# A two-layer graph network on one core: gathered tiles in two groups of seven instead of three groups of five

## The chip, the cores and the metric

One core of a Trainium2 chip runs the whole kernel. The metric is the device time in microseconds (us) of one execution, as the median of several runs; one further execution was profiled, and its trace is what the rows below come from. Engines are called as in the profile: PE (TensorE; PEld is its weight load), DVE (VectorE), ACT (ScalarE), POOL (GpSimd), SP (SyncE).

## What is computed

The graph has 12,500 nodes with 128 features and 412,500 edges, sorted by their target. Cut to what matters, the reference is:

```python
h = relu(layernorm(x))                       # layer 0
msg = where(edge_type == 0, h[src] @ W_data.T + b_data, h[src] @ W_ctrl.T + b_ctrl)
x = x + relu(segment_sum(msg, dst) + h @ W_self.T + b_self)
h = relu(layernorm(x))                       # layer 1
x = x + segment_sum((h @ W_in.T)[src], dst) + deg[:, None] * (h @ W_out.T)
```

The kernel sums the features of the source nodes first and multiplies by the weights afterwards, once per target node. What costs time is the sum over the edges.

## The kernel before, in words

**Tables.** The features of a layer are held as three bf16 parts (high, middle, low) of 128 columns each, 384 columns per node, in HBM (`tables[l]`) and in SBUF (`tab`). Nodes are taken in 98 blocks of 128; edges lie in tiles of 128, some 33 of them per block.

**Two ways of summing.** The first blocks of a layer (`GATHERED`: 56 in layer 0, 38 in layer 1) are summed by gathering. For each tile of 128 edges POOL issues an indirect DMA (L580) that brings 128 rows of 384 columns from the table into `rows`; DVE builds a 0/1 matrix `hot` that says which edge goes to which target (`make_hot`, L1130); PE multiplies the three parts by it and accumulates in `bank_g` (`add_group`, L667: three matmuls per tile, six where a tile straddles two pairs of blocks). The planner has 1,860 gathered tiles in layer 0 and 1,266 in layer 1. The other blocks are summed densely: DVE marks rows and columns (`mark`, L1142 and L1144), PE turns the marks into a 128-column strip of an adjacency matrix (`build`, L720), ACT copies it out (L961), and PE multiplies the matrix with the table in SBUF (`dense`, L737, 98 matmuls of 384 columns for each half block in layer 0, or block in layer 1).

**Steps.** All engines run through the same list of steps, in program order and without a scheduler: 16 steps for each dense sum, 1,360 steps in layer 0 and 976 in layer 1, and some before and behind. In a step PE does first the gathered groups that are due, then small turns and the ends of finished blocks, then one build and about six dense matmuls. A planner (`Plan`) spreads the groups evenly over the steps: `due[g] = 8 + g * (S - 12) // groups`. DVE builds the `hot` of a group three steps ahead of its due step, before it makes the marks of that step.

**Groups and ring.** Gathered tiles are handled in groups of `GROUP` = 5: one `make_hot` per group, one wait of PE per group for the landing of its gathers, one semaphore update after its last matmul (`s.added`). `rows` and `hot` have room for `RINGS` = 3 groups. POOL waits before a group until the group three before it was added; DVE waits likewise in `make_hot`:

```python
for g in range(plan.groups):                                   # POOL, L573
    while n < len(plan.fetch) and plan.fetch[n][0] - 4 <= plan.due[g]:
        fetch(n)
        n += 1
    if g >= RINGS:
        pool.wait_ge(s.added, g - RINGS + 1)
    for t in plan.group_tiles(g):
        pool.indirect_dma_start(...)                           # L580
```

**Other work in those queues.** POOL also fetches the edge list of a block (`fetch`, L565: 98 in layer 0, 60 in layer 1). DVE unpacks a list at step f (`unpack`, L1154 to L1177), and for a dense block PE turns it in step f + 1 (`turn_list`, L685). At the first step of each dense sum PE waits until ACT has copied the last sum out of `bank_d` (L735, L899). A general path (for graphs that the windows don't cover) is in the code and isn't taken here. Between the layers POOL waits for all stores of layer 0, and layer 1 starts with its own gathers.

**What follows from the due steps.** The step at which a pair of blocks ends (`pair_step`, one after the due step of its last group), the fetches and the ends of blocks are placed by the due steps too.

Of the kernel before, what the change touches and what calls it, by code (L numbers as in the profile page):

```python
# [7 lines left out]
def gnn_kernel(nc, x, src, dst, etype, w_data, b_data, w_ctrl, b_ctrl, w_self, b_self, w_in, w_out, out):  # L8
# [30 lines left out]

    GATHERED = (NB * 28 // 49 // 2 * 2, NB * 19 // 49 // 2 * 2)  # L40
    KINDS = (2, 1)
    GROUP, RINGS = 5, 3
    PACKS = 4
    MARKS, AHEAD = 4, 2

# [1274 lines left out]
```

How the kernel before makes its waits and increments, by code:

```python
        def wait(eng, semaphore, n):  # L386
            eng.wait_ge(semaphore, n)
            if not isinstance(n, int):
                eng.sem_inc(s_apart[eng.engine], 1)
# [1 line left out]
        def either_path(eng, fast, general):  # L391
            eng.wait_ge(s_covered, 1)
            with eng.If(eng.value_load(covered[0:1, 0:1], min_val=0, max_val=1) == 1):
                fast()
            with eng.Else():
                general()
# [4 lines left out]
        @block.sync  # L401
        def _(sp):
            sp.wait_ge(s_x_pad, 1)
            for c in range(XCH):
                n0, n1 = XB[c], min(XB[c + 1], NB - 1)
                sp.dma_start(tab_x[:, n0:n1, 0:F],
                             x[n0 * P:n1 * P, :].rearrange("(n p) f -> p n f", p=P)).then_inc(s_x[c], 16)
            sp.dma_start(tab_x[0:LAST, NB - 1, 0:F], x[(NB - 1) * P:N, :]).then_inc(s_x[XCH - 1], 16)
            pk_rows = pk.rearrange("(c p) e -> p c e", p=P)
            sp.wait_ge(s_edges[0], PIECES)
            sp.dma_start(pk_rows[:, :, 0:P], raw[0].rearrange("p (c e) -> p c e", e=P)).then_inc(s_packed, 16)
            sp.wait_ge(s_edges[3], PIECES)
            sp.dma_start(pk_rows[:, :, P:P + HALF],
                         nxt_i.bitcast(fp32).rearrange("p (c e) -> p c e", e=HALF)).then_inc(s_packed, 16)
            sp.wait_ge(s_pay, 2)
            pay = raw[2].rearrange("p (c e) -> p c e", e=P)
            sp.dma_start(pk_rows[:, :, P + HALF:2 * P + HALF], pay).then_inc(s_packed, 16)
```

## Time and profile before

| what | us |
|---|---|
| median of 3 runs | 4440.64 |
| lowest and highest run | 4433.56 and 4442.63 |
| the profiled execution's own time | 4440.43 |
| span of its instructions | 4438.4 |
| around the span | 2.0 |

By the profile's busy shares PE was busy for 92% of the span, DVE for 79%, POOL for 72%, ACT for 53%, and the DMA engines for about a third. A share is an average over stages: layer 0 runs from about 190 to 2747 us, layer 1 from about 2750 to the end, and they have to be read apart. POOL's share leaves out the time between two of its DMA instructions, which the profile calls "issue".

### The profile page before, as it was taken

To read this page: it belongs to the slowest core of one execution; us is meant where nothing else is said; L and a number is where in the kernel's file an instruction comes from. 1 tells how busy PE (TensorE), PEld (TensorE's weight loads), DVE (VectorE), ACT (ScalarE), POOL (GpSimd) and SP (SyncE) were. 2 spreads that over 40 slices of the span, in tenths; PEclk is the share of its full clock that TensorE was granted. 3 is DMA by queue.
4 is the path that set the end of the run, shared out by engine and by line. 5 is a ranking of instruction groups with operands and counts; after the bars stand their busy time and mean duration, and the time that the engine had idled before them with its cause. 6 is when DMAs were issued, how large, how long until landed. Compare 5 with 4: busy or idle time off the path is not lost.

```text
span 4438.4 us, 102927 instructions
## 1 busy us (share of the span) xinstructions
PE 4103.0 (92%) x42000; PEld 2506.4 (56%) x42000; DVE 3509.9 (79%) x8092; ACT 2334.0 (53%) x3663; POOL 3188.3 (72%) x3360
## 2 busy tenths in 40 slices
PE   0399999999999999999999996999999999999999
PEld 0255555555555555555555554566656565656665
DVE  5678777787788778778777875888888888888886
ACT  4445555555555555555555553555555555555554
POOL 4377777777777777777777775777777777777776
PEclk9599999999999999999999998999999999999999
DMA  7223333333333333333333334433333333333332
GB/s 198 73 82 91 94 88 89 93 91 90 89 90 93 90 90 92 90 92 90 91 89 92 90 89 118 124 93 91 91 93 91 91 93 91 91 91 94 90 90 78
DMA packets 289371, 417.62 MB, mean 94 GB/s; under 512 B 70913, under 2 KB 228895, under 8 KB 288895
## 3 DMA queue, kind: packets, MB, share of 16 engines
q0 software_dynamic: 160160, 338.57, 27.1%
q1 hardware_dynamic: 121784, 66.09, 5.2%
q10 hardware_dynamic: 6951, 6.30, 0.6%
q8 instruction: 336, 5.51, 0.5%
q14 instruction: 140, 1.15, 0.1%
HBM read 373.52 MB, written 37.20 MB: 93 GB/s over the span
## 4 chain that ended last, share of the span: by engine, by line
PE 53%; POOL 24%; issue 9%; DVE 8%; ACT 3%; ACTq 1%; DMA 0%; POOLq 0%; DVEq 0%; SPq 0%
PE bank_d L737 33%; POOL arena L580 23%; PE bank_g L667 10%; PE banks_m L720 8%; DVE arena L1144 1%; POOL arena L565 1%; DVE arena L1142 1%; ACT arena L961 1%; ACT arena L899 1%; DVE arena L1130 1%; ACT arena L862 1%; ACTq L824 1%; PE bank_a L694 0%; PE bank_b L703 0%; DVE tab L1053 0%
## 5 line engine op out<-in xcount | busy, mean ns | idle before, releaser
L580 POOL DMA_INDIRECT arena<-table,idx x3126 | 2971.9, 951 | 1023.3 <-issue 924.1
L737 PE MATMUL bank_d<-tab,arena 128*128 128x384 bf16 x14112 | 2696.4, 328 | 36.1 <-ACT arena L899 35.1
L961 ACT ACTIVATE arena<-banks_m 128x784 bf16<-128x784 f32 x2304 | 1912.2, 830 | 1511.4 <-PE banks_m L720 1457.3
L737 PEld LDWEIGHTS bank_d<-tab,arena 128*128 128x128 bf16 x14112 | 1196.5, 98 | 955.3 <-issue 263.6
L1142 DVE TENSOR_TENSOR arena<-iota_ps,arena 128x256 bf16<-128x256 f32 (+1 forms) x2304 | 1220.6, 530 | 335.4 <-PE banks_m L720 302.9
L1144 DVE TENSOR_TENSOR arena<-iota_ps,arena 128x392 bf16<-128x392 f32 x2304 | 1279.4, 555 | 0.0
L720 PE MATMUL banks_m<-arena 64*128 64x98 bf16 (+1 forms) x13056 | 808.1, 226 | 49.7 <-ACT arena L961 36.3
L667 PE MATMUL bank_g<-arena 128*128 128x192 bf16 (+29 forms) x12753 | 763.2, 212 | 24.8 <-DMA arena<-table,idx 23.0
L667 PEld LDWEIGHTS bank_g<-arena 128*128 128x128 bf16 x12753 | 709.7, 97 | 118.2 <-issue 27.1
L720 PEld LDWEIGHTS banks_m<-arena 64*128 64x128 bf16 x13056 | 352.2, 95 | 580.6 <-ACT arena L961 419.8
L1130 DVE TENSOR_TENSOR arena<-iota_ps,rel 128x960 bf16<-128x960 f32 (+1 forms) x626 | 592.0, 946 | 3.2
L1183 DVE TENSOR_TENSOR d_sum<-arena 128x128 f32<-128x128 f32 x144 | 42.5, 295 | 319.3 <-ACT arena L899 307.2
L565 POOL DMA_INDIRECT arena<-pk,list_at x158 | 150.1, 950 | 108.0 <-issue 74.6
L922 ACT ACTIVATE arena<-bank_a 64x128 f32<-64x128 f32 x204 | 55.5, 272 | 150.1 <-PE bank_a L686 146.9
L931 ACT ACTIVATE arena<-bank_a 128x128 f32<-128x128 f32 x196 | 54.4, 277 | 136.3 <-PE bank_a L694 132.7
L899 ACT ACTIVATE arena<-bank_d 128x384 f32<-128x384 f32 x144 | 70.8, 491 | 58.1 <-PE bank_d L737 58.1
L533 POOL TENSOR_TENSOR arena<-arena,tab 128x256 f32<-128x256 f32 x49 | 35.4, 726 | 80.5 <-ACT tab L866 75.6
L685 PE MATMUL bank_a<-ident,arena 128*128 128x128 f32 x102 | 30.4, 298 | 65.8 <-DVE arena L1177 65.8
L1201 DVE SCALAR_TENSOR_TENSOR arena<-bias,count,bank_b 128x128 f32<-128x128 f32 x98 | 33.8, 345 | 61.2 <-issue 56.7
L629 PE MATMUL banks_m<-ident,arena 128*128 128x128 f32 x30 | 6.8, 397 | 78.8 <-ACT arena L848 39.5
L1154 DVE SCALAR_TENSOR_TENSOR arena<-arena,node 128x192 f32<-128x192 int32 x158 | 64.8, 410 | 16.0 <-DMA arena<-pk,list_at 16.0
L694 PE MATMUL bank_a<-ident_b,tab 128*128 128x128 bf16 x588 | 65.0, 219 | 5.1 <-ACT arena L908 2.2
(133 smaller groups left out, 1594.6 us busy)
## 6 DMA issues: line engine op xcount, KB each, us to landing
arena<-table,idx POOLq DMA_INDIRECT x3126
table<-tab SPq DMA_DIRECT2D x7, 1344.0 KB, 5.6
table<-arena SPq DMA_DIRECT2D x98, 96.0 KB
tab<-table SPq DMA_DIRECT2D x7, 1344.0 KB, 17.1
x<-arena SPq DMA_DIRECT2D x98, 64.0 KB
arena<-x SPq DMA_DIRECT2D x98, 64.0 KB
arena<-in_x_dram SPq DMA_DIRECT2D x97, 64.0 KB
out_dram<-arena SPq DMA_DIRECT2D x97, 64.0 KB
```

Of the source, the lines that this page charges most:

```text
L565: pool.indirect_dma_start(out=pack[:, i % PACKS, :], out_offset=None, in_=pk, in_offset=bass.IndirectOffsetOnAxis(ap=list_at[:, m:m + 1], ...
L580: pool.indirect_dma_start(out=rows[:, g % RINGS * GROUP + t % GROUP, :], out_offset=None, in_=tables[l], in_offset=bass.IndirectOffsetOnAx ...
L667: last = pe.matmul(bank_g[p % 2][:, to:to + (c1 - c0) * y], rows[:, at, a * F:(a + 1) * F], hot[:, at, c0 * y:c1 * y], start=(a == 0 and p ...
L694: last = pe.matmul(bank_a[:, 0:P], mine[:, a * F:(a + 1) * F], ident_b[:, :], start=(a == 0), stop=(a == 2))
L720: last = pe.matmul(bank_m[hf][:, n * nc_:(n + 1) * nc_], is_row[at, s_ % MARKS, n, :], is_col[at, s_ % MARKS, n * nc_:(n + 1) * nc_], star ...
L737: last = pe.matmul(bank_d[:, 0:RW], adj[q % 2][:, b * P:(b + 1) * P], tab[:, b, :], start=(b == 0), stop=(b == NB - 1))
L899: act.activation(d_sb[:, :], bank_d[:, 0:RW], ACT.Copy).then_inc(s.dense_out, 1)
L961: act.activation((adj0, adj1)[l][q % 2].rearrange("p c (h d) -> p c h d", h=2)[:, :, :, n * j:n * j + n], banks_m[:, :, 0:n * nc_].rearran ...
L1130: dve.tensor_tensor(hot[:, at:at + n, 0:c], iota_w[:, 0:c].unsqueeze(1).to_broadcast([P, n, c]), (rel0, rel1)[l][:, ts[0]:ts[0] + n].unsqu ...
L1142: dve.tensor_tensor(is_row[:, s_ % MARKS, 0:n, :], iota_r.unsqueeze(1).to_broadcast([P, n, P]), rc[:, i % 2, 0, pr:pr + n].unsqueeze(2).to ...
L1144: dve.tensor_tensor(is_col[:, s_ % MARKS, 0:n * nc_].rearrange("p (n c) -> p n c", n=n), iota_c[l].unsqueeze(1).to_broadcast([P, n, nc_]), ...
L1154: after(dve.scalar_tensor_tensor(out=arena[:, V_AT:E_AT], in0=pack[:, k, 0:W3].bitcast(i32), scalar=node[:, m:m + 1], in1=pack[:, k, W3:2 ...
```

## The change

The change alters two constants. Tiles per group go from 5 to 7, groups in the ring from 3 to 2; the tiles in the ring go from 15 to 14.

```diff
     GATHERED = (NB * 28 // 49 // 2 * 2, NB * 19 // 49 // 2 * 2)
     KINDS = (2, 1)
-    GROUP, RINGS = 5, 3
+    GROUP, RINGS = 7, 2
     PACKS = 4
     MARKS, AHEAD = 4, 2
```

By the planner's formulas the groups go from 372 to 266 in layer 0 and from 254 to 181 in layer 1. The due steps lie 5 or 6 apart instead of 3 or 4. The last group of layer 0 has five tiles in both versions and is due at step 1350 instead of 1352; that of layer 1 has six tiles instead of one and is due at step 966 instead of 968. POOL and DVE wait for the group two before instead of three before. The number of gathers, of matmuls and of elements that DVE compares stays as it is.

## Rows read from the trace of the kernel before

**Rows 1.** Windows: start:end, length, busy us (instructions) by engine, PE clock, DMA.

```profile
300.00:2716.00 2416.00, 2347.59 (x21375) 1408.95 (x21376) 1921.15 (x4808) 1291.46 (x2028) 1780.81 (x1873) 1.00 0.32 90
3000.00:4400.00 1400.00, 1359.48 (x16572) 843.13 (x16570) 1169.41 (x2404) 757.45 (x1112) 1059.75 (x1117) 1.00 0.33 91
```

**Rows 2.** Groups by line, POOL, 300 to 2716 us: busy, mean ns | idle, releasers.

```profile
L580 POOL DMA_INDIRECT arena<-table,idx x1780 | 1693.5, 951 | 607.0 <-issue 516.8 <-PE bank_g L667 90.2
L565 POOL DMA_INDIRECT arena<-pk,list_at x93 | 88.3, 949 | 28.4 <-issue 28.4
```

**Rows 3.** The same, POOL, 3000 to 4400 us (layer 1).

```profile
L580 POOL DMA_INDIRECT arena<-table,idx x1068 | 1014.3, 950 | 325.6 <-issue 325.6
L565 POOL DMA_INDIRECT arena<-pk,list_at x49 | 46.5, 948 | 14.9 <-issue 14.9
```

**Rows 4.** Waits of PE, 300 to 2716 us: total us, times, longest us.

```profile
PE bank_a L685 <- DVE arena L1177: 26.6, 25, 2.4
PE banks_m L720 <- ACT arena L961: 20.0, 26, 0.8
PE bank_d L737 <- ACT arena L899: 19.6, 50, 0.7
```

**Rows 5.** Waits of PE, 2790 to 4400 us (layer 1), the longest.

```profile
PE bank_g L667 <- DMA arena<-table,idx: 23.0, 37, 1.6
```

**Rows 6.** Timeline of PE, layer 0, a step without and one with a group.

```profile
1503.35 0.34 PE L720 MATMUL banks_m<-arena 64*128 64x196 bf16 x4
...
1504.71 0.34 PE L720 MATMUL banks_m<-arena 64*128 64x196 bf16 x4
...
1505.97 1.40 PE L667 MATMUL bank_g<-arena 128*128 128x192 bf16 x15
1507.31 0.34 PE L720 MATMUL banks_m<-arena 64*128 64x196 bf16 x4
```

**Rows 7.** Groups by line and shape, DVE's make_hot: busy, mean ns | idle.

```profile
L1130 DVE TENSOR_TENSOR arena<-iota_ps,rel 128x960 bf16<-128x960 f32 x372 | 427.6, 1150 | 2.2
L1130 DVE TENSOR_TENSOR arena<-iota_ps,rel 128x480 bf16<-128x480 f32 x253 | 164.1, 649 | 0.9
```

**Rows 8.** Timeline, layer 0: hot, unpack of a list, PE's turn of it.

```profile
896.94 1.15 DVE L1130 TENSOR_TENSOR arena<-iota_ps,rel 128x960 bf16<-128x960 f32 x1
...
898.81 0.41 DVE L1154 SCALAR_TENSOR_TENSOR arena<-arena,node 128x192 f32<-128x192 int32 x1
...
900.87 0.29 DVE L1177 CAST arena<-arena 128x256 f32<-128x256 int32 x1
...
901.22 0.33 PE L685 MATMUL bank_a<-ident,arena 128*128 128x128 f32 x1 [0.48 <-DVE arena L1177]
```

**Rows 9.** Timeline, start of layer 1: gathers, third list fetch, first add, ring wait.

```profile
2752.97 0.95 POOL L580 DMA_INDIRECT arena<-table,idx  x1 [0.30 <-issue]
...
2771.79 0.98 POOL L565 DMA_INDIRECT arena<-pk,list_at  x1 [0.30 <-issue]
...
2774.00 1.38 PE L667 MATMUL bank_g<-arena 128*128 128x96 bf16 x15
...
2775.66 0.95 POOL L580 DMA_INDIRECT arena<-table,idx  x1 [2.89 <-PE bank_g L667]
```

**Rows 10.** Timeline, layer 1: last gather of a group, and its add.

```profile
3549.60 0.95 POOL L580 DMA_INDIRECT arena<-table,idx  x1 [0.31 <-issue]
...
3552.78 1.09 PE L667 MATMUL bank_g<-arena 128*128 128x22 bf16 x30
```

**Rows 11.** Waits of POOL, 2790 to 4400 us: ring waits after the first.

```profile
POOL arena L580 <- PE bank_g L667: 1.9, 3, 1.3
```

**Rows 12.** Timeline, end of layer 1: last gather and last two adds.

```profile
4416.24 0.95 POOL L580 DMA_INDIRECT arena<-table,idx  x1 [0.30 <-issue]
...
4417.73 0.52 PE L667 MATMUL bank_g<-arena 128*128 128x22 bf16 x15 [0.22 <-DVE arena L1130]
...
4422.17 0.22 PE L667 MATMUL bank_g<-arena 128*128 128x2 bf16 x3
```

## The prediction

> **What bounds the kernel now.** I read the windows first, one for each layer's steady stretch [rows 1]: PE is busy for 2347.6 of 2416 us in layer 0 (97.2%) and for 1359.5 of 1400 in layer 1 (97.1%), at full granted clock (1.00, the 2.4 GHz level). So both look bound by PE. The second view, POOL's groups by line, tells them apart. In layer 0 [rows 2] the busy and "issue" times of gathers and list fetches make 1693.5 + 516.8 + 88.3 + 28.4 = 2327 us, and 90.2 us more are waits for PE: the ring is full, PE sets the pace, POOL has 3.7% to spare. In layer 1 [rows 3] the same sum is 1014.3 + 325.6 + 46.5 + 14.9 = 1401 of 1400 us with no wait at all: here POOL is the bound, with (1014.3 + 325.6) / 1068 = 1.255 us per gather. PE's 2.9% of idle time there is the counterpart. The third view is PE's waits: in layer 0 [rows 4] none is for a gather, and the three named ones (lists from DVE 26.6 us, ACT's copies of strips 20.0, ACT's copy of a sum 19.6) are all there is; in layer 1 [rows 5] the longest is for gathers, 23.0 us in 37 waits. The change keeps the count of gathers, matmuls and compared elements, so it can only act through what is paid per group, through where a burst falls in the order, and through the depth of the ring.
>
> **Per group on PE: nothing.** In layer 0 a step without a group takes 1504.71 - 1503.35 = 1.36 us, one with a group 1507.31 - 1504.71 = 2.60 [rows 6], so five tiles cost 1.24 us, 0.083 for each of 15 matmuls. The 15 last 1.40 us from the first start to the last end, and the last alone is about 0.24 of that (1.40 less 14 x 0.083), so the group costs what its matmuls cost: switching to it and back takes 0 to 0.04 us. With 106 groups fewer in layer 0 that is 0 to -4 us; I take 0, because the pitch explains the whole 1.24. A group of seven then costs 7/5 x 1.24 = 1.74 us.
>
> **Per group on DVE.** 960 elements take 1150 ns and 480 take 649 [rows 7]: 1.044 ns an element and 148 ns for each instruction. Seven tiles take 148 + 1344 x 1.044 = 1.55 us in layer 0 (0.40 longer) and 0.85 in layer 1. DVE saves 106 x 0.148 = 15.7 us over layer 0 and 73 x 0.148 = 10.8 over layer 1. DVE is busy for 1921 of 2416 us in layer 0 [rows 1], so most of this is spare time that it gains, worth nothing. It reaches PE only where PE waits for DVE, at the lists [rows 4]. There a hot can stand just ahead of the unpack, in the same step of DVE: 1.15 us of hot, then marks, then the unpack, and PE waits 0.48 us for its end [rows 8]. That happens where a group is due three steps behind the unpack. By the planner's formulas this holds for 15 of the 41 lists behind the first in layer 0 now, and for 9 after the change. Hot ahead of an unpack thus goes from 15 x 1.15 = 17.3 us to 9 x 1.55 = 14.0. If all of that came through, PE would gain 3.3 us; I take half, **-1.5 us**. The bounds are -26.6 (all list waits go) and 25 x 0.40 = +10 (each of today's waits gets the longer hot).
>
> **Copies of the sums.** At the first matmul of a dense sum PE waits 19.6 / 50 = 0.39 us for ACT [rows 4], unless other work stands just before it. A group is due at that step in 22 of 83 cases now and in 16 after (planner), so six more waits come: **+2.3 us**. The strips' 20.0 us stay: DVE's marks and ACT's copies catch up while PE adds a group, for longer and less often.
>
> **The ring, layer 0.** A tile takes 2416 / 1780 = 1.357 us [rows 2], so seven take 9.5. Two groups before a slot is needed again are 19.0 us. In that time POOL must see the add end (0.28 us: 2774.00 + 1.38 to 2775.66, [rows 9]), issue seven gathers (8.78) and its share of list fetches (7 x 116.7 / 1780 = 0.46), the last must land, and PE must add (1.74). The landing isn't shown by itself; it is bounded by 0 and by the shortest time from the end of a group's last gather to its add, 3552.78 - 3550.55 = 2.23 us [rows 10]; I take 2.2. The sum is 13.5 of 19.0 us: 5.5 to spare, against 10.1 before (3 x 5 x 1.357 less 10.3). One or two list fetches of 1.25 us come at once, so 5.5 should do. POOL's waits for PE stay near 90 us, since PE sets the time: **0 us**.
>
> **The ring, layer 1.** POOL issues without a stop, so each wait for the ring goes straight to the end. After the last gather of a group POOL has 8.78 us of other gathers to issue; in that time PE must start the add (2.23 us later here), finish it (1.09 x 7/5 = 1.53), and be seen (0.28) [rows 10]. That is 4.0 us, 4.7 to spare. The latest case that I saw is the last add, 4422.17 - 4417.19 = 5.0 us behind its gather [rows 12]; with 1.8 on top it still leaves 2.0. So no wait in the steady stretch. At the start there is one. Two lists and 15 tiles now precede the third list at 2771.79, and POOL waits until 2775.66 [rows 9]. After the change 14 tiles end at 2752.97 + 14 x 1.255 = 2770.5 and the list at 2771.8; the first add of seven ends at 2774.00 + 1.93 = 2775.93, and POOL goes on at 2776.2, one tile and 0.55 us behind: +1.8. Of the later ring waits, 1.9 us in three [rows 11], about 1.0 is more than the usual gap of 0.3, and these go, since the next add is done before POOL has issued seven more. POOL's last gather so ends 0.8 later, at 4418.0. The tail gives it back: the last group has six tiles and is due two steps earlier. It lands by 4420.2, takes 0.52 x 6/5 = 0.62 us, and two steps of (4422.17 - 4418.25) / 4 = 0.98 us bring PE to 4422.8, against 4422.4 at the end of the last add now [rows 12]: **+0.4 us**.
>
> **Other edits.** DVE's wait for the ring is satisfied: it builds a hot three steps ahead of the due step, when the group two before, due 10 steps ahead, is long added. The first group needs seven tiles instead of five, 2.5 us later, and PE reaches its first add in layer 1 only some 15 us after five have been issued (2752.97 + 6.3 to 2774.00) [rows 9]. SP and ACT issue what they issued, the pair's copy moves by a step or two: 0.
>
> **Sum:** 4440.4 - 1.5 + 2.3 + 0.4 = **4441.6 us** for the profiled execution. This execution stands 0.2 us under the median of the runs, so I predict **4441.0 us**: no change that can be measured. About 0.2% (9 us) is what a measurement can tell from no change; the three runs differ by as much.
>
> **Rivals.** (a) *The longer hot lands on PE, slower.* Place: the lists of layer 0, L685. If hot stands in the way of most unpacks, each of the 41 lists costs 0.40 us more: +16.4 instead of -1.5, 4459 us. It decides once the step of the hot coincides with the unpack for more than today's 15. For it: these waits are the largest of PE in layer 0 [rows 4], and [rows 8] shows one. Against it: by the due steps there are 9. The Trainium skill (Perfetto Trace Analysis, section Optimizing Scalar/DVE Operations) says that where Vector is not saturated but causes bubbles on other engines, breaking instructions up may let work end sooner; by that rule this change goes the wrong way. The trace shows such bubbles, and not yet what their length hangs on. Chance 8%.
>
> (b) *The ring is too short, slower.* Place: POOL's wait before a group in layer 1. If PE's add comes later than 7 us behind the gather (8.78 less 1.8), POOL stops. Priced by what layer 0 shows: 90.2 us in some 356 groups [rows 2], 0.25 us a group, in 181 groups +45 us: 4486. For it: spare time halves. Against it: the 2.0 to 4.7 us above. The Trainium skill (Perfetto Trace Analysis, section Optimization Strategy) says that the same gap repeating on the engine that should be saturated can mean too few buffers; POOL shows no such gap in layer 1 now [rows 3], and no row here shows a ring of two. Chance 6%.
>
> (c) *DVE paces layer 0 more than its waits show, faster.* PE's waits for ACT's strips hang on marks, and marks on DVE. If the 15.7 us that DVE saves came through in full, in place of the -1.5: 4427 us. For it: 20.0 us of strip waits and 26.6 of list waits are there to be cut [rows 4]. Against it: DVE has 20% idle time. Chance 15%.
>
> (d) *Nothing moves.* The group costs PE nothing now, so the change could do just nothing: 4440.6 us. It lies inside the forecast.
>
> **How the numbers follow.** Forecast, with (d): 71%, with its own range from 4430 to 4451 (the bounds of the list waits are the widest term, and a few microseconds of them are likely). Of that, 65 points lie within 0.2%, 3 below and 3 above. Faster is then 15 + 3 = 0.18, slower 8 + 6 + 3 = 0.17, same 0.65. The range 4425 to 4456 takes in (c) and part of (a), and leaves out (b).
>
> **What would show it.** Right: 266 hots of about 1.55 us and 181 of 0.85; in layer 1 gathers at 1.255 us without waits for PE but the first, then some 4.4 us (2771.8 to 2776.2); in layer 0 PE without waits for gathers, list waits near 25 us, sum waits near 22. Wrong: POOL waiting for PE in the middle of layer 1, PE waiting for gathers in layer 0, or list or strip waits that change by over 10 us.

## The result, and the profile after

The changed kernel takes 4451.26 us (median; 4447.78 to 4456.20), the kernel before, run beside it, 4439.85 (4433.56 to 4442.63). The ratio is 1.0025, with a 95% interval from 1.0017 to 1.0034: **slower by 11 us**. That is inside the range from 4425 to 4456 and on the wrong side of "no change", by little: 0.25% against the 0.2% that was taken for the least that a measurement can tell. The profiled execution took 4448.05 us, 7.6 more than the profiled one of before. What the traces below account for is these 7.6 us, not the 11 of the medians.

The window of layer 0, and then POOL's groups by line (300 to 2716 us, then 3000 to 4400), against [rows 1 to 3]:

```profile
300.00:2716.00 2416.00, 2341.01 (x21339) 1402.30 (x21340) 1922.26 (x4700) 1285.38 (x2023) 1777.51 (x1871) 1.00 0.32 90
```

```profile
L580 POOL DMA_INDIRECT arena<-table,idx x1778 | 1690.7, 951 | 610.4 <-issue 516.1 <-PE bank_g L667 94.4
...
L580 POOL DMA_INDIRECT arena<-table,idx x1066 | 1012.7, 950 | 325.0 <-issue 325.0
```

Little moved on POOL. In layer 0 its waits for the ring went from 90.2 to 94.4 us, so PE still sets the pace. In layer 1, from 3000 us on, it waits for nothing, and a gather still takes (1012.7 + 325.0) / 1066 = 1.255 us. PE is where to look: in layer 0 it is busy for 6.6 us less in these 2416 than in [rows 1]. Its waits from 300 to 2716 us (total us, times, longest us), against [rows 4]:

```profile
PE banks_m L720 <- ACT arena L961: 26.1, 35, 1.6
PE bank_d L737 <- ACT arena L899: 24.0, 61, 0.4
PE bank_a L685 <- DVE arena L1177: 21.2, 14, 3.0
```

The same three waits stand there, in another order. Strips went from 20.0 to 26.1 us, sums from 19.6 in 50 waits to 24.0 in 61, lists from 26.6 in 25 to 21.2 in 14, with a longest of 3.0 instead of 2.4. There is no wait for a gather. DVE's `make_hot` by shape, against [rows 7], has the lengths that were worked out:

```profile
L1130 DVE TENSOR_TENSOR arena<-iota_ps,rel 128x1344 bf16<-128x1344 f32 x265 | 410.9, 1550 | 2.4 <-DVE cells L1216 0.2
L1130 DVE TENSOR_TENSOR arena<-iota_ps,rel 128x672 bf16<-128x672 f32 x180 | 152.7, 848 | 0.3
```

**What an uncovered sum costs.** The timeline of PE holds an ordinary step without a group and, behind it, the first step of a dense sum without one (start, us, instruction, idle time before it):

```profile
822.66 0.34 PE L720 MATMUL banks_m<-arena 64*128 64x196 bf16 x4
822.94 1.31 PE L737 MATMUL bank_d<-tab,arena 128*128 128x384 bf16 x7
824.18 0.34 PE L720 MATMUL banks_m<-arena 64*128 64x196 bf16 x4
824.92 1.14 PE L737 MATMUL bank_d<-tab,arena 128*128 128x384 bf16 x6 [0.40 <-ACT arena L899]
```

From the start of the build to the start of the dense matmuls it is 822.94 - 822.66 = 0.28 us in the one and 824.92 - 824.18 = 0.74 in the other. The step loses 0.46 us, where the bracket shows 0.40: idle time counts from the modelled end of the matmul ahead (822.66 + 0.34 = 823.00 in the first step), and that lies 0.06 us behind the start that the next one has there (822.94). So a wait that comes often is better measured from start to start.

**Layer 1.** The third list is no longer the place of the only real ring wait. Gathers of POOL that waited for PE, with the first adds of PE, in order of time, against [rows 9]:

```profile
2758.40 0.95 POOL L580 DMA_INDIRECT arena<-table,idx  x1 [0.30 <-issue]
...
2779.05 1.86 PE L667 MATMUL bank_g<-arena 128*128 128x96 bf16 x21
...
2781.18 0.95 POOL L580 DMA_INDIRECT arena<-table,idx  x1 [4.29 <-PE bank_g L667]
...
2796.68 2.10 PE L737 MATMUL bank_d<-tab,arena 128*128 128x384 bf16 x6
2798.58 1.60 PE L667 MATMUL bank_g<-arena 128*128 128x96 bf16 x21
...
2800.40 1.15 PE L737 MATMUL bank_d<-tab,arena 128*128 128x384 bf16 x6
2800.45 0.95 POOL L580 DMA_INDIRECT arena<-table,idx  x1 [2.03 <-PE bank_g L667]
```

The first wait is 4.29 us, as worked out. The third group's add comes at 2798.58, and POOL, with nothing left to issue, waits 2.03 us for it, which wasn't foreseen. The dense matmuls just ahead of that add run slowly: from 2760 to 2799 us the granted clock is 0.50 (the 1.2 GHz level), and six of them take 2.10 us, where the next six, at 1.00, take 1.15. In the second profile of the same kernel (experiment 1) the clock rises one such block earlier against the add, and the wait is 0.59 us. Split at the first gather of layer 1 (2752.97 in [rows 9], 2758.40 here), the 7.6 us are 5.4 in layer 0 and 2.1 in layer 1.

### The profile page after: what moved, and what is told of

It is laid out like the page before. It is cut to its first block, busy times and chain, and to the rows that moved or that the text cites. A ratio compares the mean times of both kernels' runs of the same rounds, so it can differ in the third digit from the quotient of the medians.

```text
span 4446.0 us, 102563 instructions
## 1 busy us (share of the span) xinstructions
PE 4101.9 (92%) x42000; PEld 2491.4 (56%) x42000; DVE 3516.9 (79%) x7913; ACT 2329.0 (52%) x3663; POOL 3187.9 (72%) x3360
## 4 chain that ended last, share of the span: by engine, by line
PE 51%; POOL 27%; issue 10%; DVE 7%; ACT 4%; ACTq 1%; DMA 0%; POOLq 0%; DVEq 0%; SPq 0%
PE bank_d L737 30%; POOL arena L580 26%; PE bank_g L667 11%; PE banks_m L720 8%; POOL arena L565 1%; DVE arena L1144 1%; ACT arena L961 1%; DVE arena L1142 1%; ACT arena L862 1%; DVE arena L1130 1%; ACT arena L899 1%; ACTq L824 1%; PE bank_b L703 0%; PE bank_b L704 0%; PE bank_b L705 0%
## 5 line engine op out<-in xcount | busy, mean ns | idle before, releaser
L667 PE MATMUL bank_g<-arena 128*128 128x192 bf16 (+29 forms) x12753 | 735.7, 212 | 20.8 <-DMA arena<-table,idx 19.3
L667 PEld LDWEIGHTS bank_g<-arena 128*128 128x128 bf16 x12753 | 696.4, 98 | 91.6 <-issue 38.5
L1130 DVE TENSOR_TENSOR arena<-iota_ps,rel 128x1344 bf16<-128x1344 f32 (+1 forms) x447 | 565.5, 1265 | 2.7 <-DVE cells L1216 0.2
L1053 DVE TENSOR_TENSOR tab<-arena,tab 128x256 bf16<-128x256 f32 x49 | 41.5, 865 | 33.0 <-ACT tab L879 32.8
```

The lines of the kernel that those rows point to most:

```text
L667: last = pe.matmul(bank_g[p % 2][:, to:to + (c1 - c0) * y], rows[:, at, a * F:(a + 1) * F], hot[:, at, c0 * y:c1 * y], start=(a == 0 and p ...
L1130: dve.tensor_tensor(hot[:, at:at + n, 0:c], iota_w[:, 0:c].unsqueeze(1).to_broadcast([P, n, c]), (rel0, rel1)[l][:, ts[0]:ts[0] + n].unsqu ...
```

## The experiments

All were timed beside the kernel before; the ratios are to it, with their 95% interval. The kernel before took 4436.07 us beside experiments 1 to 4, 4435.76 beside 5 to 8 and 4434.88 beside 9 to 11. Two kinds of them move groups to chosen steps, by a few lines behind the formula of the due steps. "Times" is the median of the runs.

**1. The changed kernel again.** No edit.

> The changed kernel as it is, beside the kernel before on one chip. Its first profile was 7.6 us longer in span, its median 11 us longer. All theories: +8 to +13 us against before. What a second profile should show if the loss is where the first one had it: in layer 0 (300 to 2716 us) PE waits for ACT's copies of sums near 24 us against 19.6, for strips near 26 against 20; layer 1 begins some 5 us later (first gather near 2758 against 2753), POOL's ring waits at its start near 5.7 us against 3.6. If this profile is slower than the first, the rows that differ between the two tell where the runs differ.

4444.94 us (4441.80 to 4454.47), before 4436.07: 1.0021 [1.0012, 1.0030]. So the loss is real. PE's waits are those of the first profile (24.0 us in 61 for sums, 21.2 in 14 for lists), and yet its profiled execution was the slowest of its runs, 6.4 us above the profiled one of the first time. Between steps 64 and 1343 of layer 0 PE is busy for 2333.8 us, against 2327.0 in the first profile. What differs is TensorE's clock, in short stretches (windows of this run):

```profile
350.00:361.00 11.00, 9.92 (x84) 5.94 (x81) 9.32 (x24) 5.04 (x8) 7.55 (x9) 1.00 0.34 93
361.80:368.60 6.80, 6.02 (x25) 2.59 (x26) 5.35 (x16) 2.89 (x6) 2.77 (x3) 0.50 0.27 75
```

The section at the end comes back to it.

**2. The hot of seven tiles as two instructions, of four and three.**

```diff
-            dve.tensor_tensor(hot[:, at:at+n, 0:c], ...).then_inc(s.hot, 1)
+            for a, e in ((0, 4), (4, n)) if n > 4 else ((0, n),):
+                last = dve.tensor_tensor(hot[:, at+a:at+e, 0:c], ...)
+            last.then_inc(s.hot, 1)
```

> Groups of seven in a ring of two, but DVE builds each hot in two instructions of four and three tiles (about 0.98 and 0.77 us instead of one of 1.55); 447 more instructions at 0.148 us each, 39 us of them in layer 0. Theory that the longer hot costs (rival a): it doesn't help much either, since both halves stand one behind the other in DVE's order and the marks come after both; +0.15 us on each of some 14 list waits, so +2 us or more against the changed kernel, up to +10 if DVE's time itself is scarce. Theory that the uncovered copies of sums cost: no change, within 3 us of the changed kernel. Theory of the ring depth: no change.

4449.03 us (4446.86 to 4452.11): 1.0030 [1.0019, 1.0041]. No gain over the 4444.94 of the unsplit kernel on the same chip. The list waits from 300 to 2716 us stay too:

```profile
PE bank_d L737 <- ACT arena L899: 24.0, 61, 0.4
PE bank_a L685 <- DVE arena L1179: 21.4, 14, 3.0
```

Lists wait 21.4 us in 14 against 21.2 in 14. The length of one instruction isn't what delays them; the amount of DVE's work ahead of the unpack may be, and that wasn't changed: both halves still stand ahead of it. The Trainium skill (Perfetto Trace Analysis, section Optimizing Scalar/DVE Operations) says that breaking up Vector's instructions may help where Vector isn't saturated and causes bubbles on other engines; here it did not.

**3. Groups of seven, moved onto the first steps of the dense sums of layer 0.** For each such step the nearest group takes it as its due step, so 83 of 83 have one.

```diff
         self.due = [...]
+            for m in range(32, 16 * (self.Q + 1), 16) if l == 0 else ():
+                g = min(range(self.groups), key=lambda g: abs(self.due[g] - m))
+                self.due[g] = m
```

> Groups of seven in a ring of two; in layer 0 the group that is due nearest to the first step of each dense sum is moved onto that step, so that by the planner's formulas a group is added there in 83 of 83 cases instead of 16 (22 in the kernel before). Theory that the copies of sums that no group covers cost layer 0 its time: PE's waits at L737 for ACT L899 in layer 0 fall from 24 us to about 0, layer 0 is about 24 us shorter, the run about 24 us below the changed kernel, some 13 below the kernel before. Theory of the longer hot: list waits stay, so at most a few us either way from the moved phases. Theory of the ring depth: no gain, and PE waiting for gathers in layer 0 where two groups now lie three steps apart.

4421.72 us (4414.83 to 4424.42): 0.9967 [0.9955, 0.9979], 23 us under the changed kernel, and faster than the kernel before. PE's waits from 300 to 2716 us (the edit moves the line numbers by 3):

```profile
PE banks_m L723 <- ACT arena L964: 21.8, 32, 0.8
PE bank_a L688 <- DVE arena L1180: 20.0, 14, 2.5
PE bank_g L670 <- DMA arena<-table,idx: 8.1, 6, 2.9
```

The wait for ACT's copy of the sum is gone from the list. In its place stands a new wait for gathers, 8.1 us in six: where a moved group comes to lie three or four steps behind its neighbour, seven gathers aren't always there in time. Group size and ring are those of the change, so these two alone don't make it slow; the place of the groups does more.

**4. Groups of five, ring of two.** The ring's two groups without the longer group: `GROUP, RINGS = 5, 2`. The ring holds ten tiles here, four fewer than in the change.

> Groups of five, ring of two groups (ten tiles): the depth alone, with the kernel before's due steps. Theory of the ring depth: at the start of layer 1 POOL stops after ten tiles (near 2766) until the first add is seen at 2775.7, 9 us instead of 2.6, and more at the next groups, so layer 1 ends some 6 to 9 us later; in layer 0 one round of the ring (2 x 6.8 = 13.6 us) has 3.3 us to spare (0.3 + 6.6 + 2.2 + 1.2 used), so PE waits for some gathers, 2 to 10 us. Together +8 to +19 us against before. Theory of the copies of sums: as many are covered as before, no change in layer 0.

4449.41 us (4446.80 to 4451.57): 1.0030 [1.0019, 1.0041], 13 us over before. PE's waits from 300 to 2716 us, then POOL's from 2750 to 4400:

```profile
PE bank_d L737 <- ACT arena L899: 19.6, 50, 0.7
...
PE bank_g L667 <- DMA arena<-table,idx: 2.6, 4, 0.7
```

```profile
POOL arena L580 <- PE bank_g L667: 12.7, 2, 10.4
```

The sums wait as in [rows 4], to the tenth: the due steps are those of before. What a ring of ten tiles costs stands at the start of layer 1, where POOL's ring waits come to 12.7 us against 4.8 in the kernel before, and a little in layer 0, where steps 64 to 1343 take 2.4 us longer. The rest of the 13 us isn't accounted for. Fourteen tiles cost less there: 6.3 us of ring waits in the first profile of the change and 5.1 in the second. So the depth of the ring has a price, at one place, and the cover of the sums has another; the change pays little for the first.

**5. The move of experiment 3 in the kernel before** (`GROUP, RINGS = 5, 3`).

> Groups of five in a ring of three, as before, with the same move of due steps in layer 0: one group on the first step of each dense sum (83 of 83 instead of 22). Theory that the cover of ACT's copies by a group's matmuls is what counts, whatever the size of a group: PE's waits at L737 for ACT in layer 0 fall from 19.6 us to about 0, the run is about 20 us faster than before (4416 where before is 4436), and faster than or like the same move with groups of seven (14 us under before). Theory that groups of seven gained and only the phase hid it: slower than that one by 5 us or more.

4406.78 us (4403.07 to 4408.35), before 4435.76: 0.9932 [0.9919, 0.9946]. From 300 to 2716 us the sums are gone from PE's waits, and lists and strips stay near [rows 4]:

```profile
PE bank_a L688 <- DVE arena L1180: 22.3, 23, 2.6
PE banks_m L723 <- ACT arena L964: 19.5, 28, 0.8
```

And the timeline shows how the cover works, at the first step of a sum:

```profile
818.67 1.45 PE L670 MATMUL bank_g<-arena 128*128 128x140 bf16 x30
820.05 0.34 PE L723 MATMUL banks_m<-arena 64*128 64x196 bf16 x4
820.33 1.15 PE L740 MATMUL bank_d<-tab,arena 128*128 128x384 bf16 x6
```

PE adds a group first, ACT copies the last sum in that time, and from build to dense matmul it is 820.33 - 820.05 = 0.28 us, as in a step that starts no sum. From step 64 to step 1343 layer 0 takes 2363.5 us, against 2393.5 in the kernel before: 30 us, more than the 20 that the waits alone let expect. The 50 waits of [rows 4] make 50 x 0.46 = 23 of it, and the list waits, 26.6 to 22.3, another 4. The planner has 83 - 22 = 61 sums without a group there, but not all of them wait. The end of a finished block can stand ahead of a sum as well, and it covers the copy too, as in this step of the kernel before (L705 is the end of a block):

```profile
405.45 0.39 PE L705 MATMUL bank_b<-wT,arena 128*128 128x128 f32 x2
405.77 0.34 PE L720 MATMUL banks_m<-arena 64*128 64x196 bf16 x4
406.04 1.15 PE L737 MATMUL bank_d<-tab,arena 128*128 128x384 bf16 x6
```

From build to dense matmul it is again 406.04 - 405.77 = 0.27 us, without a group.

**6. Groups of seven, moved one step behind the unpack of each list of layer 0 instead.**

```diff
+            for m in range(55, 32 * (self.D - 1) - 8, 32) if l == 0 else ():
+                g = min(range(self.groups), key=lambda g: abs(self.due[g] - m))
+                self.due[g] = m
```

> Groups of seven, ring of two; in layer 0 the group due nearest to the step in which PE turns a list is moved onto that step (planner: 38 of 42 lists instead of 9), so that PE adds 1.74 us of matmuls before it asks for the list. The copies of sums stay as in the changed kernel. Theory that long list waits cost twice, by themselves and by the fall of PE's granted clock to 0.5 that stands beside waits of more than 2 us in the traces: list waits in layer 0 fall from 21 us to under 6, no stretch at 0.5 remains between 300 and 2700 us, and the run is 20 to 30 us below the changed kernel, with less spread between runs than its 8 to 13 us. Theory that the clock falls have another cause: list waits fall, the stretches at 0.5 stay, and the gain is 15 us or less.

4431.85 us (4429.80 to 4433.02): 0.9991 [0.9982, 1.0000], 13 us under experiment 1, not the 20 to 30 expected. PE's waits from 300 to 2716 us:

```profile
PE banks_m L723 <- ACT arena L964: 31.3, 46, 1.6
PE bank_d L740 <- ACT arena L902: 24.7, 62, 0.7
PE bank_a L688 <- DVE arena L1180: 6.2, 6, 1.6
```

Lists went from 21.2 to 6.2 us, and strips took 5 us of that back (26.1 to 31.3): PE, no longer held at the list, comes to the strip before ACT, which copies the turned list ahead of it. The clock doesn't fall in the middle of layer 0 here, and the runs lie within 3.2 us of one another, against 12.7 in experiment 1.

**7. Groups of seven, the due steps of layer 1 earlier.**

```diff
-            self.due = [8 + g * (self.S - 12) // self.groups for g in range(self.groups)]
+            self.due = [(8, 2)[l] + g * (self.S - (12, 6)[l]) // self.groups for g in range(self.groups)]
```

> Groups of seven, ring of two, layer 0 unchanged; in layer 1 the first group is due at step 2 instead of 8, the others are spread so that the last stays at step 966. Theory of the ring depth (layer 1 is paced by POOL, and a ring of two stops it at the start): POOL's ring waits in layer 1 fall from 5 or 6 us to under 1, its last gather ends 5 us earlier after its first one, and the run is 4 to 6 us below the changed kernel. Theory that layer 1 isn't where time was lost: within 2 us of the changed kernel.

4440.11 us (4438.42 to 4447.64): 1.0015 [1.0006, 1.0024], 4.8 us under experiment 1 as expected, though the two intervals overlap. The ring waits of layer 1 (from 2725 us on) go from 6.3 us to

```profile
POOL arena L580 <- PE bank_g L667: 1.6, 1, 1.6
```

So POOL waits 4.7 us less, and the kernel takes 4.8 us less. POOL's chain in layer 1 is its gathers, the time between them and these waits, so they go to the end in full; that the two numbers agree so closely is luck. From the first to the last gather of layer 1 this execution takes 9.2 us less than the first profile of the change: 4.7 by the waits, and 4.5 because its DMA instructions are 3 ns shorter each (mean 947 against 950 ns), which differs between executions of one kernel too. The new due steps also put a group on 13 of the 59 sums of layer 1 that can wait, where the change has none.

**8. Groups of five, ring of three, moved onto both the sums and the lists.** The list of steps is `sorted([*range(32, 16 * (self.Q + 1), 16), *range(55, 32 * (self.D - 1) - 8, 32)])`, the rest as in experiment 3.

> Groups of five, ring of three; in layer 0 one group is moved onto the first step of each dense sum and one onto the step in which PE turns a list (35 of 42). Theory of the cover: sum waits 19.6 to about 0, list waits 26.6 to under 8, the strips' waits that follow a list's copy (0.84 us each) may stay; no stretches at clock 0.5 in mid layer; 35 to 50 us below the kernel before. If the moved groups only shift the waits elsewhere: less than 25 us.

4403.43 us (4401.38 to 4407.04): 0.9929 [0.9916, 0.9943]. PE's waits from 300 to 2716 us hold no sums; lists are 6 us below experiment 5, strips 4 above, and the kernel gains 3 us, with intervals that overlap. The 32 us under before fall short of the 35 to 50 expected:

```profile
PE banks_m L723 <- ACT arena L964: 23.5, 34, 1.4
PE bank_a L688 <- DVE arena L1180: 16.2, 16, 1.5
```

**9. Only the cover taken away from the kernel before.** The 22 groups that are due at the first step of a sum in layer 0 go one step later; size and ring stay five and three.

```diff
+            self.due = [d + (l == 0 and d % 16 == 0 and d >= 32) for d in self.due]
```

> The kernel before (groups of five, ring of three) with one edit: in layer 0 the 22 groups that are due on the first step of a dense sum are moved one step later, so none of the 83 sums is covered; the list steps keep as many groups as before. Size of a group and depth of the ring stay. Theory of the cover: some 18 to 22 more waits of 0.39 us at L737 for ACT's copy, 19.6 to about 28 us, and by what the opposite move gained (29 us for 61 sums, 0.48 each) 8 to 11 us slower than before: the loss of the change without its edit. Theory that size or ring made the loss in layer 0: within 3 us of before.

4447.60 us (4442.79 to 4449.43), before 4434.88: 1.0027 [1.0016, 1.0039], 12.7 us slower. PE's waits from 300 to 2716 us:

```profile
PE bank_d L738 <- ACT arena L900: 27.2, 70, 0.4
PE bank_a L686 <- DVE arena L1178: 25.2, 25, 2.4
PE banks_m L721 <- ACT arena L962: 19.0, 24, 0.8
```

Lists and strips are those of [rows 4] within 1.4 us; of PE's waits only the sums moved, by 20 (50 to 70). Step 64 to 1343 takes 2403.2 us, 9.8 more than before, and 20 x 0.46 = 9.2. Two more falls of the clock than in the profile of before, 6.8 us at half clock, are in this too and are worth 3.4 us at most. So a loss as large as the change's appears without any change of group or ring, with 20 more waits where the change has 11. The 2.9 us between 9.8 and 12.7 aren't accounted for.

**10 and 11. Both moves and the earlier layer 1,** with groups of five and a ring of three (10), and with groups of seven and a ring of two (11).

> Groups of five, ring of three, with the moves of both kinds in layer 0 (sums and lists) and in layer 1 the first group due at step 2 and the last where it was. Theory of the ring at the start of layer 1: the kernel before loses 3.6 us there, so this gains 2 to 4 us on the run with both moves alone: 33 us under before becomes 35 to 37. Rival: groups that are added before the dense matmuls have begun only move PE's work, no gain.

> Groups of seven, ring of two, with the same three moves as the run with groups of five. If the moves cover what the change laid bare, and the ring costs its 4.5 us at the start of layer 1 alone, both sizes end within 5 us of each other, near 4400 where before is 4436. If a ring of two costs in layer 0 too once PE is faster there, PE waits for gathers in layer 0 (8 us with the sums' move alone) and this stays 8 us or more behind the run with groups of five.

The fives take 4401.35 us (4399.08 to 4402.98): 0.9924 [0.9910, 0.9938]; the sevens 4404.65 (4402.34 to 4405.51): 0.9932 [0.9919, 0.9946]. PE's waits from 300 to 2716 us, of the fives and then of the sevens:

```profile
PE banks_m L723 <- ACT arena L964: 23.8, 34, 1.6
PE bank_a L688 <- DVE arena L1180: 15.5, 16, 1.4
```

```profile
PE banks_m L723 <- ACT arena L964: 26.8, 42, 0.8
PE bank_g L670 <- DMA arena<-table,idx: 11.4, 13, 2.7
PE bank_a L688 <- DVE arena L1180: 5.4, 6, 1.4
```

With the groups where they cover, seven in two and five in three differ by 3.3 us, and the intervals overlap. The sevens have 11.4 us of gather waits that the fives don't show, and 10 us less of list waits. The fives are the fastest version of this study, 33.5 us under the kernel before (35 to 37 were expected).

A ring of three groups of seven, which would tell size and depth apart at this size, was not run.

## Why the prediction was right in its range and wrong in its terms

The time lies in the range, and "no change" did not hold: for the profiled execution +1.2 us was forecast and +7.6 measured. That the miss is no larger is in part luck, since the lists fell by more than was forecast where strips and sums rose.

**The step that failed is the copies of the sums.** The mechanism was right: a sum waits unless other work stands ahead of it, and groups of seven are due there less often than groups of five. The size was off twice. "Six more waits" were 11 in the profile (50 to 61). The prediction counted groups alone, 22 to 16 of 83; but the steps at which blocks end follow the due steps, and by the two traces a block's end stands just ahead of nine uncovered sums before and of four after, and none of these waits. And a wait was priced by the 0.39 us of the waits' view, where the step loses 0.46. So the term of +2.3 us is 11 x 0.46 = 5.1. Experiments 5 and 9 test the price from both sides: about 26 us gained beside the lists' 4 where 23 were to come by 0.46, 9.8 lost where 9.2 were.

**The strips didn't stay.** "The strips' 20.0 us stay" became 26.1 us. The argument, longer adds but fewer of them, left out where the adds stand: counted by steps in the two traces, none of the 26 waits before and the 35 after lies in a step in which a group is due. That this is the same cover is supported by experiment 6, where strips rise as list waits go. No run moved groups onto the strips alone.

**The lists moved the right way, and further.** The prediction took -1.5 us; the wait's total went down by 5.4. There are fewer of them, 14 instead of 25. Of the 15 lists that by the planner have a hot just ahead of the unpack all wait before, 18.8 us together; of the 9 after, six do, for 10.2 us. So the mean of these waits has grown from 1.25 to 1.70 us, by about the 0.40 that the hot is longer, and six waits instead of three pass 2 us, up to 2.99. The waits at the other lists rose from 7.8 us in ten to 11.0 in eight. The bounds held (-26.6 to +10).

**What this adds up to.** The windows from step 64 to step 1343, before and after:

```profile
317.50:2710.97 2393.47, 2327.42 (x21197) 1397.51 (x21196) 1905.28 (x4761) 1281.92 (x2013) 1765.31 (x1856) 1.00 0.32 91
314.81:2716.74 2401.93, 2326.98 (x21198) 1393.71 (x21197) 1910.71 (x4668) 1279.13 (x2014) 1767.03 (x1859) 1.00 0.32 90
```

The stretch is 8.5 us longer and PE no busier, so all of it is waiting. Inside these windows strips are +5.3 us (20.0 to 25.3), lists -3.4 (24.6 to 21.2), sums 12 x 0.46 = +5.5 (49 to 61 waits), and two small new waits +0.7: 8.1 of the 8.5. The start and the end of layer 0 give 3.0 back, nearly all before step 64; the two profiles of the changed kernel differ by 2.4 us in that start themselves, so this isn't the change's doing for certain.

**Layer 1: the first wait right, the second missed.** +0.4 us became +2.1. The later ring waits were to go "since the next add is done before POOL has issued seven more"; one add, at 2798.58, wasn't, behind dense matmuls at half clock, and POOL waited 2.03 us. In the second profile that wait is 0.59 us and layer 1 takes 0.2 us less than before, so the +2.1 is no more than executions differ by. And the prediction didn't count the sums of layer 1, where 17 of 59 have a group before and none after. PE's waits there, 2790 to 4400 us, before and after:

```profile
PE bank_d L737 <- ACT arena L899: 14.5, 38, 0.4
PE bank_d L737 <- ACT arena L899: 22.3, 58, 0.4
```

These 7.8 us more don't reach the end: POOL sets the pace there, and PE waits anyway.

**What held.** The hot's 1.55 and 0.85 us and its counts; PE's cost per group of nothing that shows (2327.4 and 2327.0 us busy between the same steps); POOL at 1.255 us a gather and without a ring wait in the steady part of layer 1; no gather wait in layer 0. Of the rivals, (a), the longer hot, falls as such: splitting it gave nothing, and list waits fell in total, though those behind a hot grew. (b) is seen only at the start of layer 1, where ring waits of 6.3 and 5.1 us stand against 4.8: 0.3 to 1.5 us instead of 45. The Trainium skill (Perfetto Trace Analysis, section Optimization Strategy) reads a repeated gap as a possible sign of too few buffers; here the gap doesn't repeat. (c) falls: DVE's hots of layer 0 take 410.9 us and one hot of five tiles, instead of 427.6, and PE gained nothing by it; DVE's busy time between steps 64 and 1343 didn't even fall (1905.3 and 1910.7 us).

## What to carry to other kernels

Where a fixed order of work hides another engine's latency, a new batch size moves every hiding place: count the covered steps before and after, by everything that can stand ahead of the wait, and choose them on purpose, which was worth 29 us here (experiment 5) where size and ring were worth a few. Price a wait by the time from start to start beside a like step without it. And where a queue is the bound, as POOL is in layer 1, each microsecond that it waits at its start goes to the end, while the waits of the other engines don't.

## What was not expected

**The clock falls in the middle of a stretch at 97% busy.** In layer 0 the granted clock goes from 1.00 to 0.50, the 1.2 GHz level, and comes back. Windows of the first profile of the changed kernel, and its timeline just before:

```profile
1900.00:1912.00 12.00, 11.86 (x118) 7.03 (x116) 11.45 (x35) 6.10 (x10) 9.06 (x10) 1.00 0.28 77
1915.70:1919.10 3.40, 3.40 (x38) 3.05 (x37) 3.10 (x6) 1.22 (x3) 0.00 (x0) 0.50 0.10 28
1925.00:1937.00 12.00, 11.49 (x97) 7.01 (x96) 9.38 (x25) 6.78 (x13) 8.67 (x10) 1.00 0.27 76
```

```profile
1914.22 0.33 PE L685 MATMUL bank_a<-ident,arena 128*128 128x128 f32 x1 [2.36 <-DVE arena L1177]
```

PE waited 2.36 us for a list, started again at 1914.22, and from 1915.7 to 1919.1 us it was busy throughout at half the clock. The first profile of the changed kernel has two such falls (the other beside the wait of 2.99 us), the kernel before three, beside waits of 2.01, 1.92 and 2.39. The second profile of the changed kernel, experiment 1, has four, three of them 6.8 us long. Together that is 23.9 us at half clock against 6.8, worth at most (23.9 - 6.8) / 2 = 8.5 us; step 64 to 1343 takes 5.8 us more there, with 6.8 us more of busy time on PE and no more waiting. Experiments 6, 8, 10 and 11, whose list waits from 300 to 2716 us stay at 1.6 us or less, have no fall in the middle of layer 0. In experiment 3 one of four falls stands beside a gather wait of 2.89 us, so it needn't be a list; but experiment 11 has a gather wait of 2.7 us without a fall. So the price of a long wait is more than its length, and it differs from run to run: that would explain the spread of 12.7 us in experiment 1 and of 3.2 in experiment 6, and perhaps why the medians of before and after lie 11 us apart and the profiled executions 7.6, though only one execution of each was profiled. The Trainium skill (TensorE: Matmul & The Clock Gate, Part 1) names the two levels and a monitor that chooses by PE's activity; the rows agree. Why some waits bring a fall and others of the same length don't (two of the six above 2 us in the first profile) stays open.
